# Self attention in a transformer kernel: dense stacks of 32 rows for q and k, heads stored in the order "four groups side by side"

## The reference, cut to what matters

```python
NQ = 16; NKV = 4; HD = 8
h = rmsnorm(x, ln1_w)
q = (h @ Wq + bq).reshape(batch, seq, NQ, HD)
k = (h @ Wk + bk).reshape(batch, seq, NKV, HD)
v = (h @ Wv + bv).reshape(batch, seq, NKV, HD)
q = rmsnorm(apply_rope(q, cos, sin), qn_w)
k = rmsnorm(apply_rope(k, cos, sin), kn_w)
k = jnp.repeat(k, 4, axis=2)            # four query heads share one key head
v = jnp.repeat(v, 4, axis=2)
scores = jnp.einsum('bthd,bshd->bhts', q, k) / np.sqrt(HD)
scores = jnp.where(causal[None, None], scores, -jnp.inf)
attn = jax.nn.softmax(scores, axis=-1)
out = jnp.einsum('bhts,bshd->bthd', attn, v)
gate = jax.nn.sigmoid(out @ Wg + bg)
x = x + (out * gate).reshape(batch, seq, DIM) @ Wo + bo
```

## Time and profile before

| quantity | value |
|---|---|
| time, median of 3 runs | 2042.4 us (2041.14 to 2043.27) |
| profiled execution, its own time | 2044.91 us |
| span of its trace | 2043.1 us |
| mean granted TensorE clock | 0.881 |
| PE matmul busy | 1633.6 us (80%) |
| DVE busy | 1342.5 us (66%) |
| ACT busy | 946.6 us (46%) |
| POOL busy | 778.1 us (38%) |
| copies to `qS` (L842), all three attention stages | 384 of 576 ns |
| L439, all three stages | 384 of 449 ns |
| the self attention stage | about 1089 to 1436 us of the span |

### The profile page before, as it was taken

How to read it: one execution, slowest core, us unless ns; L and a number is a source line. 1 busy time by engine, 2 the same in 40 slices (tenths; PEclk the granted TensorE clock), 3 DMA queues, 4 the chain that set the end, 5 groups by cost and what they waited for, 6 DMA issues and landing times. The chain is left out here.

```text
span 2043.1 us, 42298 instructions
## 1 busy us (share of the span) xinstructions
PE 1633.6 (80%) x14686; PEld 1274.5 (62%) x14686; DVE 1342.5 (66%) x4040; ACT 946.6 (46%) x1817; POOL 778.1 (38%) x1156
## 2 busy tenths in 40 slices
PE   5999953977799998898885899998458899998440
PEld 3666642976677777566653566665347799997330
DVE  4777753348887776677775788885546577774632
ACT  2776621533333343466663777776124444443110
POOL 2222235345300000112114677773554544442525
PEclk9999975978799999699996899999569899999565
DMA  6132202831000000000000000000057000000043
GB/s 183 50 132 91 87 12 88 252 99 39 18 1 1 0 1 1 8 8 8 8 4 1 1 2 2 2 2 2 21 147 208 15 14 14 15 14 2 25 136 87
DMA packets 60416, 91.88 MB, mean 45 GB/s; under 512 B 11587, under 2 KB 49492, under 8 KB 59668
## 3 DMA queue, kind: packets, MB, share of 16 engines
q1 hardware_dynamic: 54068, 76.67, 12.2%
q0 software_dynamic: 6144, 12.60, 2.1%
HBM read 72.71 MB, written 35.39 MB: 53 GB/s over the span
## 5 line engine op out<-in xcount | busy, mean ns | idle before, releaser
L667 DVE TENSOR_REDUCE parts<-PS 128x8 fp32r<-128x1024 f32 x192 | 234.7, 1222 | 165.8 <-PE PS L424 165.6
L865 ACT ACTIVATE P<-PS 128x1024 f32<-128x1024 f32 x192 | 197.7, 1030 | 101.4 <-PE PS L439 101.4
L842 ACT CAST qS<-PS 32x512 fp32r<-32x512 f32 x384 | 221.1, 576 | 9.6 <-PE PS L391 6.1
L272 POOL TENSOR_TENSOR ve<-mv,eps_t 128x1 f32<-128x1 f32 x160 | 33.4, 209 | 422.6 <-DVE mv L268 422.6
L1637 DVE SCALAR_TENSOR_TENSOR X<-PS,wt,X 128x128 f32 (+1 forms) x480 | 134.8, 344 | 46.3 <-PE PS L1480 38.8
L1480 PEld LDWEIGHTS PS<-w_f_w,P 128*128 128x128 f32 x1024 | 129.9, 193 | 39.3 <-issue 27.3
L1769 ACT ACTIVATE P<-PS,w_f_b 128x512 f32<-128x512 f32 x128 | 88.0, 688 | 141.4 <-PE PS L1461 140.0
L1480 PE MATMUL PS<-w_f_w,P 128*128 128x128 f32 x1024 | 141.9, 283 | 13.1 <-DVE X L1637 11.3
L439 PE MATMUL PS<-qS,kS 128*128 128x512 f32 x384 | 151.1, 449 | 1.0 <-ACT P L865 1.0
L391 PE MATMUL PS<-ident_r,parts 128*128 128x128 f32 x768 | 123.3, 294 | 25.0 <-issue 24.3
L762 POOL TENSOR_TENSOR rrs<-rsq,neg_half 128x20 f32<-128x20 f32 x32 | 114.4, 3573 | 74.4 <-DVE rsq L597 74.4
(11 more groups left out here) (299 smaller groups left out, 4238.9 us busy)
## 6 DMA issues: line engine op xcount, KB each, us to landing
tok<-hs SPq DMA_DIRECT2D x62, 128.0 KB, 3.4
hs<-yo SPq DMA_DIRECT2D x62, 128.0 KB, 4.0
P<-in_f_blob SPq DMA_DIRECT2D x12, 578.0 KB, 4.8
Y<-in_f_blob SPq DMA_DIRECT2D x11, 578.0 KB, 5.0
ctxT<-in_ctxT SPq DMA_DIRECT2D x128, 48.0 KB, 1.7
P<-in_f_blob SPq DMA_DIRECT2D x12, 450.0 KB, 4.4
Y<-in_f_blob SPq DMA_DIRECT2D x11, 450.0 KB, 4.3
w_f_w<-in_f_w SPq DMA_DIRECT2D x2, 1024.0 KB, 5.7
```

What stands on the lines that cost most here:

```text
L667: e.tensor_reduce(parts[:, it.s, 0, 8 * half:8 * half + 8, 3, 0], S_ps[:, :, :].rearrange("p i (j t) -> p (i j) t", t=T), AXX, ALU.max)\
L842: m = e.copy(qS[r, it.s % 2, :, j, :], TP[0][r, :].rearrange("p (g t) -> p g t", g=4))
L865: e.activation(P[:, it.s % 2, 8 * half:8 * half + 8, :].rearrange("p h t -> p (h t)"), ST_ps[:, :, :].rearrange("p j n -> p (j n)"), ACT.E ...
```

## The change

In the self stage the 16 heads in `qk` are stored in the order "j outer, g inner": place 4j+g holds query head 4g+j, and for k the head g. A stack matmul then puts four heads of the four different groups on 128 rows: rows 32g to 32g+31 belong to group g. For q there are four such stacks, next to each other as before, and the copy to `qS` is one copy of 128x512. For k the four stacks would be equal, so one is made: 1 stack matmul, a copy of 128x128 to `kS`, and `high` and `g_low` handle 20 heads in place of 32. In `pe_scoresT` the score matmul of group g takes 32 rows of `kS` and 32 rows of `qS`; the matmul of the causal bias in front of it keeps its 128 rows. The maximum of head place p is still written to place p, since q and k are permuted alike. The two other attention stages keep their code.

```diff
--- before.py
+++ after.py
@@ -387,7 +387,7 @@
                 m.then_inc(s_turn, 1)
 
             def turn_stack(e, it, which, done):
-                for g in range(4):
+                for g in range(1 if causal and which == 1 else 4):
                     m = e.matmul(TP[which][:, g * T:(g + 1) * T],
                                  parts[:, it.s, which, 4 * g:4 * g + 4, :, :].rearrange("p h c d -> p (h c d)"),
                                  ident_r[:, :], start=True, stop=True)
@@ -436,9 +436,12 @@
                     g = 2 * half + i
                     if causal:
                         e.matmul(ST_ps[:, i, :], ident_r[:, :], causal_k[:, :], start=True, stop=False)
-                    m = e.matmul(ST_ps[:, i, :], kS[:, it.s % 2, g, :],
-                                 qS[:, it.s % 2, g, :, :].rearrange("p j t -> p (j t)"),
-                                 start=not causal, stop=True)
+                        m = e.matmul(ST_ps[:, i, :], kS[32 * g:32 * g + 32, it.s % 2, 0, :],
+                                     qS[32 * g:32 * g + 32, it.s % 2, 0, :, :].rearrange("p j t -> p (j t)"),
+                                     start=False, stop=True)
+                    else:
+                        m = e.matmul(ST_ps[:, i, :], kS[:, it.s % 2, g, :],
+                                     qS[:, it.s % 2, g, :, :].rearrange("p j t -> p (j t)"), start=True, stop=True)
                 m.then_inc(s_st, 1)
 
             def pe_values(e, it, what):
@@ -612,11 +615,12 @@
                     e.wait_ge(s_lo, at(s_lo, 2 * (it.n - 1)))
                 if due(it.n - 1):
                     e.wait_ge(s_turn, at(s_turn, it.n - 1))
-                e.tensor_tensor(qk[:, it.s % 2, 0], ra[:, 0:H16, :],
-                                w[p + "norm"][:, 0, :].unsqueeze(1).broadcast_to([T, H16, DH]), ALU.mult)\
-                 .then_inc(s_qkf, 1)
-                e.tensor_tensor(qk[:, it.s % 2, 1].rearrange("p (g j) d -> p g j d", g=4),
-                                ra[:, H16:n_heads, :].unsqueeze(2).broadcast_to([T, 4, 4, DH]),
+                e.tensor_tensor(qk[:, it.s % 2, 0].rearrange("p (j g) d -> p g j d", j=4),
+                                ra[:, 0:H16, :].rearrange("p (g j) d -> p g j d", g=4),
+                                w[p + "norm"][:, 0, :].unsqueeze(1).unsqueeze(1).broadcast_to([T, 4, 4, DH]),
+                                ALU.mult).then_inc(s_qkf, 1)
+                e.tensor_tensor(qk[:, it.s % 2, 1].rearrange("p (j g) d -> p j g d", j=4),
+                                ra[:, H16:n_heads, :].unsqueeze(1).broadcast_to([T, 4, 4, DH]),
                                 w[p + "norm"][:, 1, :].unsqueeze(1).unsqueeze(1).broadcast_to([T, 4, 4, DH]),
                                 ALU.mult).then_inc(s_qkf, 1)
 
@@ -650,8 +654,9 @@
                 if due(it.n - RING + 1):
                     e.wait_ge(s_tq, at(s_tq, it.n - RING + 1))
                 e.wait_ge(s_qkf, at(s_qkf, (2 if causal else 1) * (it.n + 1)))
-                src = qk[:, it.s % 2].rearrange("p a h d -> p (a h) d").unsqueeze(2).broadcast_to([T, 2 * H16, 3, DH])
-                dst = parts[:, it.s, :, :, 0:3, :].rearrange("p a h c d -> p (a h) c d")
+                n = n_heads if causal else 2 * H16
+                src = qk[:, it.s % 2].rearrange("p a h d -> p (a h) d")[:, 0:n].unsqueeze(2).broadcast_to([T, n, 3, DH])
+                dst = parts[:, it.s, :, :, 0:3, :].rearrange("p a h c d -> p (a h) c d")[:, 0:n]
                 (e.copy if causal else e.tensor_copy)(dst, src).then_inc(s_hi, 1)
 
             def v_kx(e, it):
@@ -740,8 +745,9 @@
             def g_low(e, it):
                 e.wait_ge(s_hi, at(s_hi, it.n + 1))
                 for which, place in ((0, 2), (1, 1)):
-                    e.tensor_tensor(parts[:, it.s, which, :, place, :], qk[:, it.s % 2, which, :, :],
-                                    parts[:, it.s, which, :, 0, :].bitcast(F32), ALU.subtract).then_inc(s_lo, 1)
+                    n = 4 if causal and which == 1 else H16
+                    e.tensor_tensor(parts[:, it.s, which, 0:n, place, :], qk[:, it.s % 2, which, 0:n, :],
+                                    parts[:, it.s, which, 0:n, 0, :].bitcast(F32), ALU.subtract).then_inc(s_lo, 1)
 
             def g_rsqrt2(e, it):
 
@@ -831,12 +837,18 @@
                 if due(2 * (it.n - 1)):
                     e.wait_ge(s_st, at(s_st, 2 * (it.n - 1)))
                 e.wait_ge(s_tk, at(s_tk, it.n + 1))
-                e.copy(kS[:, it.s % 2].rearrange("p g t -> p (g t)"), TP[1]).then_inc(s_kS, 1)
+                if causal:
+                    e.copy(kS[:, it.s % 2, 0], TP[1][:, 0:T]).then_inc(s_kS, 1)
+                else:
+                    e.copy(kS[:, it.s % 2].rearrange("p g t -> p (g t)"), TP[1]).then_inc(s_kS, 1)
 
             def a_qS(e, it):
                 if due(2 * (it.n - 1)):
                     e.wait_ge(s_st, at(s_st, 2 * (it.n - 1)))
                 e.wait_ge(s_tq, at(s_tq, it.n + 1))
+                if causal:
+                    e.copy(qS[:, it.s % 2, 0].rearrange("p j t -> p (j t)"), TP[0]).then_inc(s_qS, 1)
+                    return
                 for j in range(4):
                     r = slice(32 * j, 32 * j + 32)
                     m = e.copy(qS[r, it.s % 2, :, j, :], TP[0][r, :].rearrange("p (g t) -> p g t", g=4))
```

## The result

The changed kernel takes 2101.6 us (median of 6 runs, 2090.1 to 2110.6) against 2041.7 us; the ratio is 1.029, with a 95% interval of 1.027 to 1.031. It is slower, as forecast, but by 60 us where 28 were forecast. The profiled execution took 2102.86 us with a span of 2101.0, 57.9 more than before.

The account below looks back on a forecast made before the run. Loops through several engines, none full, were taken to bound the stage, with PE and ACT's loop setting 10.57 us after the change. Steady +24.4, front +2.6, end +1 gave +28.0: 2070.4 us, range 2054 to 2085.

Parts of the forecast that it names:

- three loops: Self stage: ACT's queue at 9.69 us a step, POOL with DVE at 9.61, PE with ACT having 0.15 us slack.
- second loop: POOL's power, DVE's L608 waiting for it, DVE's queue to the next power: 9.61 us, none of its instructions shortened.
- L608's wait: DVE's L608 waiting for POOL's power; seen after the change, it would show the forecast wrong.
- step 1: ACT copies to qS, kS and parts: 2.27 us a step saved, of which 0.15 at most is gained.
- step 2: PE's stack matmuls: three of eight go, 0.35 us less a step on the PE and ACT loop.
- step 3: PE's scoresT: 32-row matmuls between 128-row ones make a half 1.69 us, 0.69 more; the turn behind takes 0.10 more.
- step 4: Path: scores half 0 starts 0.44 us later, scoresT half 1 runs 0.59 longer; period 9.69 becomes 10.57 us.
- the sum: Total for the program: steady part +24.4 us, steps in front +2.6, end +1; together +28.0, giving 2070.4 us.
- a granted clock of 1.0 in the steady part: Expected sign in the self stage's profile after: TensorE stays at full clock, so clock falls add nothing.
- the fourth rival: Dearer: accumulation waits (+8, 2078 us), or longer pauses lower the clock (40 us costing some 24, 2094 us); 8%.
- The two steps in front: Steps before the steady part, at mean clock 0.75: scoresT costs 1.3 us more in each, +2.6 us.
- the last steps and the item behind them: End of the stage: items without a turn, fewer copies, shorter gains from the halves; +1 us.

Follow-up runs that it names:

- e11: Kernel before the change, with DVE's v_heads moved in front of v_qk_norm; 2042.3 us, ratio 1.001.
- e1: Changed kernel with each scoresT half ordered bias, bias, 32-row score, 32-row score; 2035.6 us, ratio 0.998.
- e2: Changed kernel with scoresT's score matmul reading all 128 rows, adding four groups' scores (different output); 2033.8 us, ratio 0.996.
- e10: Changed kernel with ACT's copy to qS again in four pieces of 32 partitions; 2095.1 us, ratio 1.026.
- e9: Changed kernel plus two unread 32-row, 512-column matmuls at the end of each step, in TensorE's pause; 2119.2 us, ratio 1.041.
- e7: Changed kernel with the bias matmul also reading only its group's 32 rows, leaving out most of the causal bias; 2050.9 us, single run.
- e3: Changed kernel plus two unread 128-row, 512-column matmuls at the end of each step, in TensorE's pause; 2073.0 us, ratio 1.016.
- e5: e1 with added ACT copies (three of 512 columns, one of 128) before the second exponential; 2086.9 us, ratio 1.021.
- e6: e2 with added ACT copies (three of 512 columns, one of 128) before the second exponential; 2063.8 us, ratio 1.012.
- e12: e6 with 416 in place of 128 columns in the last added ACT copy; 2078.0 us, ratio 1.020.
- e4: Kernel before the change, with two more ACT copies (128x512, 128x256) behind those to qS; 2065.5 us, ratio 1.014.

## Why the prediction was right in its sign and wrong in its size

**Loops.** That three loops lie within 0.15 us of each other was right: ACT's queue at 9.69 (e11 leaves it there), POOL's power at 9.61 as worked out, 9.57 measured (e1, e2), PE with ACT closest behind. The terms of the second loop, 3.54, 0.04 and 6.01, give 9.59 and not 9.61. And the two rows chosen for it show more than the trace does: before the change, L608 starts 0.03 to 0.07 us after the power's end in about two steps of three and 0.33 to 0.36 after it in the third, and in the steady part DVE does not stand idle in front of it. So this loop was nearly closed, and not closed. L608's wait in e1 and e2 is the one that was named.

**ACT, step 1.** 0.59, 0.27 and 0.59 against 0.586, 0.266 and 0.60. Hidden, as said (e10).

**Stacks, step 2.** Five matmuls in place of eight; on the chain they have 0.70 us and had 1.05, the 0.35 less that were counted.

**ScoresT, step 3.** 1.69 forecast, 1.68 measured. That it is the passage, and not the 32 rows, is shown by e9 (0.34 and 0.32 for two of them in a row), by e7 (no passage inside, 0.66 for the half) and, in part, by e1. Two pages were weighed there. The Trainium skill's page TensorEngine Tiling (Array Packing), section Key Properties, has a change of tiling mode drain the engine. The trace agrees as far as it can: loads are no longer ahead, and L439 takes 0.43 where 0.23 had been. The Trainium skill's page TensorE: Matmul & The Clock Gate has, in its closing table, a single matmul with K=32 take the time of one with K=128. That is so for the two of e9 (0.66 us, and 0.64 for two of 128 rows in e1), and it is not so between 128-row neighbours (0.43 against 0.23).

**The path, step 4.** 10.57 us forecast for the step, 10.57 measured at full clock. Its parts are off by up to 0.05: scores half 0 starts 0.39 later where 0.44 was forecast, and scoresT half 1 takes 1.78 to its end where 1.75 was. They cancel, so the last hundredth is luck; the path and its terms are not.

**The failed step is the sum's clock.** The sum put the steady part at a granted clock of 1.0, "+24.4 us", and the profile after was to show "a granted clock of 1.0 in the steady part". It is 0.92 from 1160 to 1400 us. In the 26 steps the falls cost 20.2 us, beside the 22.9 us of the longer step (24.4 forecast). The loss was put at nothing in the sum and left to the fourth rival, with 8% and 24 us for 40 us of low clock; measured in the 26 steps are 47.6 us at 0.50. The rival's price is right only if its 40 us are the time of the work at full clock: 40 us of the trace at 6.3 matmuls a us in place of 10.0 are 15 us lost. No row of before could say when the clock would fall. But the change takes away work from TensorE and spreads the rest over a longer step, and the earlier trace rows showed what a low clock costs in this very stage, so more than 8% was due to it. e3 shows the other side: with the clock held, 2073.0 us against the forecast 2070.4 (its profiled execution 2068.7).

The sum is off at both ends too. The two steps in front take 6.4 us more for 2.6 forecast, and the clock first rises 23.7 us later than before (1146.6 against 1122.9). In the last steps and the item behind them, with several low stretches where there was one, it is 9.5 us for 1 forecast. How much of these two sums is the clock's was not measured apart.

The spread of the runs fits: the six runs have mean clocks from 0.862 (2110.6 us) to 0.874 (2090.1 us). With their spans, these clocks are 526 and 582 us at half clock in the whole program, 56 us more for 20.5 us of time: 0.37 us for each us at half clock, and the profile's 20.2/47.6 is 0.42.

What stays open: in what proportion the rows that a matmul reads and the passages between tiles lower the clock. e9 against e3 and e5 against e6 and e12 differ in both. Nor do these runs show where between a step of 9.57 (e1, no fall in its profile) and 10.45 (e5) a kernel with paired 32-row matmuls begins to fall.

## What to carry to other kernels

A narrow matmul between wide ones costs the passage: group the narrow ones, those of different row groups next to each other so that they run side by side, and look at the distance between starts in the trace where the kernel already changes tile, since those distances gave the new half to 0.01 us. Before a saving is counted, close every loop that passes the place and write down its period; here three lay within 0.15 us, and only the exchange that opened the second one together with the first brought more than 0.2%. And when a change makes TensorE do less in a longer step, ask what it does to the granted clock: here it cost nearly as much again as the longer step itself.

## What the runs showed of the hardware that was not expected

- Work added to TensorE made the program faster: two 128-row matmuls of 512 columns a step, in a pause, took 2101.6 us down to 2073.0 (e3). The same with 32 rows took it to 2119.2 (e9).
- The granted clock does not follow the profile's busy share: 203 us of 240 with a clock of 0.92 (e5), 192 with 0.97 (e12), 206 with 1.00 (e4), 226 with 0.92 (the changed kernel, whose longest pause is 0.8 us).
- Weights are loaded 0.23 us ahead of their matmul where both matmuls read 128 rows (before) and where both read the same 32 (e9), and together with it where the row count changes (after).
- In e7 the program order of a half is bias, score, bias, score; the trace records the starts of both biases within 0.01 us of each other at 1309.91 and of the scores at 1310.24 and 1310.26. By that record the second bias, on another row group, started before the first score, which stands in front of it.
